# Gated cross-attention and routed feed-forward: mask and row maxima in one product of 115 rows, and a stationary first layer

## What is computed

```python
x = x + tanh(g_xattn) * xattn(layernorm(x), ctx, ctx, mask)        # 16 heads of 16
x = x + tanh(g_ffn) * ffn(layernorm(x))

# xattn: q, k, v = projections with biases
scores = einsum('bhqd,bhkd->bhqk', q, k) / sqrt(16)
scores = where(mask, -1e15, scores)
out = (softmax(scores) @ v) @ Wo + bo

# ffn: a router picks 3 of 8 zones for each image, with weights w that sum to 1
z = gelu(x @ Wa[e]) @ Wb[e]                                        # 256 -> 1024 -> 256
return x + sum over the three zones of z * w[e]
```

## Time and profile before

| | us |
|---|---|
| median of 3 runs (383.84 to 386.05) | 385.92 |
| the profiled execution | 384.96 |
| its span, first to last instruction | 383.2 |
| TensorE busy in it | 344.4 |
| VectorE, ScalarE, GpSimd busy | 177.0, 195.7, 158.5 |

### The profile page before, as it was taken

How to read it: one execution, slowest core, us unless ns; L and a number is a source line. 1 busy time by engine, 2 the same in 40 slices (tenths; PEclk the granted TensorE clock), 3 DMA queues, 4 the chain that set the end, 5 groups by cost and what they waited for, 6 DMA issues and landing times.

```text
span 383.2 us, 8751 instructions
## 1 busy us (share of the span) xinstructions
PE 344.4 (90%) x3060; PEld 267.8 (70%) x3060; DVE 177.0 (46%) x559; ACT 195.7 (51%) x398; POOL 158.5 (41%) x219
## 2 busy tenths in 40 slices
PE   2775896997999989989998878999999999999995
PEld 2542674875767768767776655888788887888875
DVE  4337455375475684765859352233332222222221
ACT  3334565564565657656775665344553434344341
POOL 4946767368466596674988681000000000000000
PEclk9968999899999999999999899999999999999999
DMA  7967648259367476572664130110101010101000
GB/s 171 280 182 198 173 120 235 86 139 208 106 174 196 126 211 178 145 220 70 191 173 138 60 118 3 35 38 24 38 2 38 0 39 2 39 0 38 2 12 14
DMA packets 32921, 40.40 MB, mean 105 GB/s; under 512 B 9992, under 2 KB 26688, under 8 KB 32880
## 3 DMA queue, kind: packets, MB, share of 16 engines
q1 hardware_dynamic: 26176, 22.07, 22.5%
q0 software_dynamic: 4784, 16.98, 15.1%
q10 hardware_dynamic: 1920, 0.79, 0.8%
HBM read 33.09 MB, written 6.74 MB: 104 GB/s over the span
## 4 chain that ended last, share of the span: by engine, by line
PE 71%; DMA 7%; DVE 7%; POOL 5%; issue 3%; ACT 3%; SPq 2%; ACTq 0%
PE bank L1184 17%; PE bank L1156 16%; PE bank L1020 5%; PE bank L1012 5%; PE bank L1166 5%; PE bank L970 4%; PE bank L960 4%; PE bank L994 3%; DMA stage<-in_L_ffn_Wa 3%; PE bank L980 3%; PE bank L974 3%; POOL wa L445 3%; PE bank L1037 2%; DVE bank L745 2%; DMA stage<-in_L_ffn_Wb 2%
## 5 line engine op out<-in xcount | busy, mean ns | idle before, releaser
L745 DVE CUSTOM_DVE_ANT_0 bank<-bank,maskb 112x375 f32<-112x375 f32 x128 | 67.8, 569 | 36.6 <-PE bank L960 36.5
L912 DVE SCALAR_TENSOR_TENSOR stage<-bank,wbc,stage 128x448 f16<-128x448 f32 x48 | 32.8, 684 | 85.8 <-ACT stage L708 85.8
L1156 PE MATMUL bank<-wa,ctxT 128*112 x288 | 70.0, 379 | 2.1 <-issue 2.1
L1184 PE MATMUL bank<-wb,stage 128*112 x576 | 67.0, 273 | 1.2 <-DVE stage L912 1.2
L1184 PEld LDWEIGHTS bank<-wb,stage 128*112 128x112 f16 x576 | 63.4, 130 | 4.1 <-issue 1.4
L527 ACT ACTIVATE pT<-bank 125x448 f32<-125x448 f32 x96 | 49.1, 539 | 21.9 <-PE bank L980 21.7
L708 ACT ACTIVATE stage<-bank,wbc 128x448 f16<-128x448 f32 x48 | 30.2, 630 | 54.3 <-PE bank L1166 54.2
L1156 PEld LDWEIGHTS bank<-wa,ctxT 128*112 128x112 f16 x288 | 35.7, 130 | 19.1 <-issue 2.3
L445 POOL TENSOR_TENSOR wb<-stage,wb 128x512 f16<-128x512 f32 x32 | 36.7, 1157 | 22.3 <-ACT wb L626 22.2
L445 POOL TENSOR_TENSOR wa<-stage,wa 128x512 f16<-128x512 f32 x32 | 36.7, 1156 | 21.8 <-ACT wa L626 21.6
L960 PE MATMUL bank<-kst,qbd 128*112 128x375 f16 x128 | 36.0, 344 | 10.3 <-DVE peaks L745 7.1
(11 more groups left out here) (113 smaller groups left out, 440.8 us busy)
## 6 DMA issues: line engine op xcount, KB each, us to landing
stage<-in_L_ffn_Wa POOLq DMA_DIRECT2D x16, 512.0 KB, 4.9
stage<-in_L_ffn_Wb POOLq DMA_DIRECT2D x16, 512.0 KB, 5.5
kst<-k_scr SPq DMA_DIRECT2D x64, 93.8 KB, 3.5
k_scr<-k_hl SPq DMA_DIRECT2D x16, 187.5 KB
ctx_s<-in_ctx SPq DMA_DIRECT2D x8, 336.0 KB
qbd<-q_scr SPq DMA_DIRECT2D x32, 56.0 KB, 3.2
xa<-in_x SPq DMA_DIRECT2D x8, 112.0 KB, 2.6
q_scr<-q_hl SPq DMA_DIRECT2D x32, 28.0 KB
```

Of the source, the lines that this page charges most:

```text
L745: v.tensor_tensor_reduce(out=bank[0:SQ, e, 0:SK], in0=bank[0:SQ, e, 0:SK], in1=maskb[:, b % 2, 0:SK], scale=-1.0, scalar=3.0e38, op0=ALU.a ...
L1156: ins = T.matmul(o, x2b[:, b % 2, xs * DT * SQ + t * SQ:xs * DT * SQ + (t + 1) * SQ], wa[:, bass.ds(e * (4 * CHUNK) + ws * (2 * CHUNK) + t ...
L1184: ins = T.matmul(o, hT[:, hs * FT * SQ + f * SQ:hs * FT * SQ + (f + 1) * SQ], wb[:, bass.ds(e * (4 * CHUNK) + ws * (2 * CHUNK) + f * D, D) ...
```

## The change

- **Mask and maxima in one product.** The mask tile gets three rows of ones below its 112, and the moving operand `rq` (115 rows, 448 columns, two buffers) holds four identities side by side and, below them, three rows with the maxima's parts of the four heads. The four products with `pick` go. The three rows lie on other partitions than the 12 transposed ones, so SyncE writes `ms` to DRAM (`write_max`) and reads three rows of it into `rq` for each group of tiles (`move_max`).
- **First scores a slot ahead.** Pairs 0 and 1 of image n now stand in slot 0 of iteration b, pairs 6 and 7 in slot 3. `row_max`, `split_max` and MX0 move with them; K0 and K1 come before Q; `mask_bias` moves to slot 3 of the iteration before.
- **Fully masked rows.** The negated minimum starts at 1e14 instead of 3e38, a floor. `vp` and `pT` get a 126th row in the last third: the row of V sums (times 2^-100) against a row of ones. For it the two copies of the transposed context also accumulate their row sums into column 376 (the one of VectorE becomes a multiply with accumulation).
- **First layer stationary.** VectorE copies the chosen zone's 4096 fp16 columns of `wa` to a fixed place, `wst3` and `wst1` (the attention weights' and part of `qbd`'s memory), and `g1(u)` streams x (112 columns) against 48 stationary blocks of 128 x 128. The result is already transposed, in four banks taken in turn; `ht` goes. ScalarE's gelu reads it to `h_w` and a second activation makes the high half (`hidden`), VectorE the low (`low`). `hT` has two buffers. TensorE's order is g1(u+1), g2(u). The last step of an image is done one unit later (`put_out`).

The diff, cut to its core:

```diff
     every = (
-        (("V0", n), ("XT", m), ("V1", n), ("MX1", b), ("CX0", m), ("CX1", m)),
-        (("Q", m), ("OT", o), ("K0", m), ("K1", m), ("X2T", b - 2)),
-        (("ON", o),),
-        (("MX0", n), ("OP", o)),
+        (("V0", n), ("XT", m), ("V1", n), ("CX0", m), ("CX1", m), ("MX1", b)),
+        (("K0", m), ("K1", m), ("Q", m), ("OT", o), ("X2T", b - 2)),
+        (("MX0", n), ("ON", o)),
+        (("OP", o),),
     )
...
+            def write_max(b, h):
+                if there(b):
+                    sp.wait_ge(s["ms_done"], 2 * b + h + 1)
+                    sp.dma_start(m_scr[b, h, :, :, :], ms[:, :, :]).then_inc(s["m_written"], 16)
+
+            def move_max(b, g):
+
+                if there(b):
+                    sp.wait_ge(s["m_written"], 16 * (2 * b + g // 2 + 1))
+                    need(sp, s["pe_st"], tile(b, g, 0) - KC)
+                    sp.dma_start(rq[SQ:KQ, g % 2, :].rearrange("c (j q) -> c j q", j=4),
+                                 m_scr[b, g // 2, :, g % 2, :].rearrange("(c j) q -> c j q", j=4)).then_inc(rq_in[g % 2], 16)
...
             sp.dma_start(wqkvo[:, 2, :, :], view_w(Wv)).then_inc(s["wv_loaded"], 16)
             for b in range(-2, B):
                 n, m, o = b + 1, b + 2, b - 1
+                move_max(b, 1)
                 read_q(n, 1)
                 read_k(n, 1)
                 load_xr(o)
                 load_mask(m)
                 load_x(m + 1)
-
+                write_max(b, 1)
                 load_ctx(m + 1)
+                move_max(b, 2)
+                write_k(m, 0)
+                write_k(m, 1)
+                move_max(b, 3)
                 write_q(m)
                 store_r(b - 2)
-
-                write_k(m, 0)
-                write_k(m, 1)
                 store_x2(b - 2)
+                write_max(n, 0)
...
+                read_k(m, 0)
                 read_q(m, 0)
-                read_k(m, 0)
+                move_max(n, 0)
...
-            def gelu(u, hf):
-
-                act.wait_ge(s["g1_done"], u * 2 + hf + 1)
-                need(act, s["ht_full"], u * 2 - 1 + hf)
-                a.activation(h_f[:, hf * 512:(hf + 1) * 512], bank[0:SQ, hf, :], ACT.Gelu_apprx_tanh,
-                             scale=1.0 / WSCALE).then_inc(s["gelu_done"], 1)
-
-            def ht_hi(u, hf):
-                if hf == 0:
-                    act.wait_ge(s["wbc_done"], 1 if u // TOPK < ROUTES[1][0] else 2)
-                act.wait_ge(s["ht_full"], u * 2 + hf + 1)
-                need(act, s["g2_done"], u)
-                a.activation(hT[:, hf * 448:hf * 448 + 448], bank[:, 2 + hf, 0:448], ACT.Copy,
-                             scale=wbc[:, u:u + 1]).then_inc(s["hthi_done"], 1)
+            def hidden(u):
+
+                act.wait_ge(s["wbc_done"], 1 if u // TOPK < ROUTES[1][0] else 2)
+                need(act, s["g2_done"], u - 1)
+                for hf in range(2):
+                    act.wait_ge(s["g1_done"], 2 * u + hf + 1)
+                    need(act, s["htlo_done"], 2 * u - 1 + hf)
+                    cols = slice(hf * QUAD, (hf + 1) * QUAD)
+                    a.activation(h_w[:, cols], bank[:, 2 * (u % 2) + hf, 0:QUAD], ACT.Gelu_apprx_tanh, scale=1.0 / WSCALE).then_inc(s["gelu_done"], 1)
+                    act.wait_ge(s["gelu_done"], 2 * u + hf + 1)
+                    a.activation(hT[:, u % 2, cols], h_w[:, cols], ACT.Copy, scale=wbc[:, u:u + 1]).then_inc(s["hthi_done"], 1)
...
             for b in range(-2, B):
                 n, m, o = b + 1, b + 2, b - 1
-                row_max(b, 6)
-                row_max(b, 7)
-                split_max(b, 1)
+                row_max(n, 0)
+                row_max(n, 1)
                 cx_copy(m)
                 if b == B - 1:
                     route_logits(0)
 
-                row_max(n, 0)
-                row_max(n, 1)
-                if b == -2:
-                    dve.wait_ge(s["wq_scaled"], 2)
-                q_lo(m)
-                o_rows(o)
-                if b == -2:
-                    dve.wait_ge(s["bk_loaded"], 16)
-                k_lo(m, 0)
-                result(b - 2)
-                k_lo(m, 1)
-                if b == B - 1:
-                    route_top(0)
-
                 row_max(n, 2)
                 row_max(n, 3)
                 split_max(n, 0)
+                if b == -2:
+                    dve.wait_ge(s["wq_scaled"], 2)
+                    dve.wait_ge(s["bk_loaded"], 16)
+                k_lo(m, 0)
+                k_lo(m, 1)
+                q_lo(m)
+                o_rows(o)
+                result(b - 2)
+                if b == B - 1:
+                    route_top(0)
+
+                row_max(n, 4)
+                row_max(n, 5)
                 x2_lo(b - 2)
                 ln1_stats(m + 1)
 
-                row_max(n, 4)
...
+            def copy_weights(u):
+
+                if u == ROUTES[1][0] * TOPK:
+                    dve.wait_ge(s["idx_loaded"], 32)
+                e = dve.value_load(idx_row[0:1, u:u + 1], min_val=0, max_val=NZ - 1)
+                need(dve, s["g1_done"], 2 * u)
+                v.tensor_copy(wst3, wa[:, bass.ds(e * (4 * CHUNK), 3 * CHUNK)]).then_inc(s["wst_done"], 1)
+                v.tensor_copy(wst1, wa[:, bass.ds(e * (4 * CHUNK) + 3 * CHUNK, CHUNK)]).then_inc(s["wst_done"], 1)
+
+            def low(u):
+                dve.wait_ge(s["wbc_done"], 1 if u // TOPK < ROUTES[1][0] else 2)
+                for hf in range(2):
+                    dve.wait_ge(s["hthi_done"], 2 * u + hf + 1)
+                    cols = slice(hf * QUAD, (hf + 1) * QUAD)
+                    v.scalar_tensor_tensor(out=hT[:, u % 2, (2 + hf) * QUAD:(3 + hf) * QUAD], in0=h_w[:, cols], scalar=wbc[:, u:u + 1],
+                                           in1=hT[:, u % 2, cols], op0=ALU.mult, op1=ALU.subtract).then_inc(s["htlo_done"], 1)
+
...
+            dve.wait_ge(s["idx_loaded"], 16)
+            dve.wait_ge(s["hi_done"], NPART)
+            dve.wait_ge(s["lo_done"], NPART)
+            full(dve, ("V1", B - 1))
+            dve.wait_ge(s["pe_st"], tile(B - 1, 0, 0))
+            copy_weights(0)
             for u in range(B * TOPK):
                 b, k = u // TOPK, u % TOPK
-                if k == 0:
-                    dve.wait_ge(s["wbc_done"], 1 if b < ROUTES[1][0] else 2)
-                for hf in range(2):
...
+                if u + 1 < B * TOPK:
+                    copy_weights(u + 1)
+                low(u)
...
-                    T.matmul(o[0:w, :].rearrange("k (j q) -> k j q", j=4), maskb[:, b % 2, c * CK:c * CK + w],
-                             bass.AP(ident_b, 0, [[SQ, SQ], [0, 4], [1, SQ]]), start=True, stop=False)
+                    if c == 0:
+                        pe.wait_ge(rq_in[g % 2], 16 * (2 * b + g // 2 + 1))
+                    T.matmul(o[0:w, :], maskb[0:KQ, b % 2, c * CK:c * CK + w], rq[0:KQ, g % 2, :], start=True, stop=False)
                     for i in range(2):
                         p = 2 * g + i
-                        T.matmul(o[0:w, i * 2 * SQ:(i + 1) * 2 * SQ].rearrange("k (e q) -> k e q", e=2),
-                                 kst[:, b % 2, p * SK + c * CK:p * SK + c * CK + w], qbd[:, b % 2, :, p, :],
-                                 start=False, stop=False)
-                    if c == 0:
-                        pe.wait_ge(s["ms_done"], 2 * b + g // 2 + 1)
-                    for j in range(4):
-                        ins = T.matmul(o[0:w, j * SQ:(j + 1) * SQ], pick[:, j, 0:w], ms[:, g, :],
-                                       start=False, stop=(j == 3))
+                        ins = T.matmul(o[0:w, i * 2 * SQ:(i + 1) * 2 * SQ].rearrange("k (e q) -> k e q", e=2),
+                                       kst[:, b % 2, p * SK + c * CK:p * SK + c * CK + w], qbd[:, b % 2, :, p, :],
+                                       start=False, stop=(i == 1))
                     ins.then_inc(s["pe_st"], 1)
...
             for b in range(-2, B):
                 for slot in range(4):
-                    n, p = (b, 6) if slot == 0 else (b + 1, 2 * slot - 2)
                     st_tile(b, slot, 0)
-                    s1(n, p)
+                    s1(b + 1, 2 * slot)
                     st_tile(b, slot, 1)
                     pv(b if slot else b - 1, (slot - 1) % COUPLES)
                     st_tile(b, slot, 2)
-                    s1(n, p + 1)
+                    s1(b + 1, 2 * slot + 1)
                     for name in slot_uses(b, slot):
...
-            def g1(u, e, hf):
+            def first(ws, t, f):
+                i = ws * DT + t
+                return wst3[:, i * CHUNK + f * 128:i * CHUNK + f * 128 + 128] if i < 3 else wst1[:, f * 128:f * 128 + 128]
+
+            def g1(u):
 
                 b, k = u // TOPK, u % TOPK
-                if k == 0 and hf == 0:
+                if k == 0:
                     pe.wait_ge(x2b_loaded[b % 2], 16 * (b // 2) + 16)
-                need(pe, s["gelu_done"], u * 2 - 1 + hf)
-                o = bank[0:SQ, hf, :]
```

(35 more changed lines are left out.)

168 lines of the change are left out of this document (95 added, 73 removed).

## The result

| | before | after |
|---|---|---|
| median of the runs (range) | 385.99 us (383.84 to 387.86) | 397.01 us (394.97 to 397.76) |
| profiled span | 383.2 us | 396.0 us |
| first tile of scores | 39.05 us | 50.72 us |
| slot 0 of image 6 begins | 189.04 us | 219.71 us |
| first feed-forward product | 230.80 us | 262.75 us |

The changed kernel is slower, by a ratio of 1.0285 (95% interval 1.0231 to 1.0339). Some executions of any of these kernels fall in a slower state: medians are of all runs, ratios of the others alone. 366 was forecast, so 31 us are missing, and the table says where: the feed-forward stage gave 19.1 us of the 24, and the attention stage cost 32 us where +6 was expected.

What follows compares the result with a forecast made beforehand. TensorE was taken to bound both stages, with a loop of DMAs close behind in attention. Attention +6 and feed-forward -24 on the profiled 384.96 us gave 366 us; its own range was 361 to 373, the wider one 350 to 380.

Steps and rivals of the forecast that it cites:

- the 24: Feed-forward stage: first layer without transposes, a unit of 4.94 us instead of 5.99, 24 us saved in all.
- +6: Attention stage in all: start +8, six iterations +2, end -4, so 6 us longer.
- rival (d): Feed-forward first layer paced by weight loads, 80 ns a product: +11 instead of -23, 402 us; chance 0.06.
- rival (e): Feed-forward weight copy goes by elements, 4.7 us, VectorE becomes the bound, 7.1 us a unit: 416 us; chance 0.08.
- by bytes: Feed-forward weight copies on VectorE, timed by bytes rather than elements: 2.6 us, just hidden behind the second layer.
- The stall itself: Attention, before slot 0: TensorE waits for the maxima, last in SyncE's queue, a new 3.6 us an iteration.
- the chain of 6.5 us from the end of x2_lo: SyncE's queue before slot 0: x2 store, maxima write, k and q reads, maxima read landing, 6.5 us.
- The clock: Attention: TensorE at half clock after stalls, 1.7 us lost each, in five of six iterations, 8.5 us.
- The rest of the iteration: Attention slots shortened by removed maxima products: 6.5, 6.75, 3.3 and, with the stall, 7.7, 24.2 us against 25.0.
- The end: From slot 0 of image 6 to the first feed-forward product: products removed, maxima waits and first copy added, -4 us.
- (c): Attention: maxima for slots 2 and 3 also late under weight traffic, +12 to +18: 378 to 385 us; chance 0.10.
- the eight small terms of the queue: Attention: the stall's length is a sum of eight small terms of SyncE's queue, named the likeliest error.

Runs made afterwards that it cites:

- e12: e7 with expert numbers stored ahead of x2 and the first weight copy ahead of a residual, in the last iteration: 363.9 us, ratio 0.9423 to the kernel before.
- e7: Kernel before with only the change's feed-forward parts, and two weight parts prepared in every slot, where slot 3 had one: 369.6 us, ratio 0.9653.
- e2: Changed kernel with the maxima left out of the scores and their two transfers through DRAM removed: 387.82 us, ratio 1.0073 to the kernel before.
- e9: Changed kernel with 64 unread products on TensorE just before it waits for slot 0's maxima: 389.41 us, ratio 1.0095 to the kernel before.
- e17: Kernel before with next x's factors at the start of slot 3 (GpSimd) and its normalisation behind slot 0's third exponential (ScalarE): 375.92 us, ratio 0.9707.
- e11: Kernel before with new feed-forward stage, 115-row product fed by transposes to partitions 96 to 98 without DRAM, smaller exponential and moving-tile rings: 372.7 us, ratio 0.9679.
- e18: Changed kernel with nothing but the normalisation order of e17: 396.26 us, ratio 1.0249 to the kernel before.
- e10: e2 with q ahead of k throughout, and stores of residual and x2 behind the reads of both in all iterations but the last: 375.18 us, ratio 0.9689.
- e14: e11 with the early first weight copy of e12, two weight parts in every slot and the order of e17: 353.57 us, ratio 0.9161.
- e13: e12 with the normalisation order of e17: 353.12 us, ratio 0.9175 to the kernel before.

## Why the prediction was wrong

**Feed-forward: right in mechanism and unit, 5 us short.** The first layer takes 2.36 us (2.32 forecast; 48 times 48 ns is 2.30), 49 ns a product, so rival (d) fell. The two copies take

```profile
L943 DVE COPY wqkvo<-wa 128x3072 f16 x24 | 23.2, 965 | 42.7 <-PE bank L1214 38.3 <-issue 4.3
L944 DVE COPY qbd<-wa 128x1024 f16 x24 | 10.1, 419 | 0.0
```

0.965 + 0.419 = 1.38 us and are hidden in most units; rival (e) fell. The bound "by bytes" of 2.6 us was twice too dear. By the Trainium skill (VectorE: DVE Perf Modes, The perf-mode tier table) it would have been an estimated 1.3; the trace agrees. The second row of the wait list has 10.9 us for the copy. 6.3 of them stand ahead of the first product and count below, under the end of attention. The missing part of this stage is the other 4.6, in four early units, where VectorE's leftover work of attention stands ahead of the copy, and the first unit's clock: its 48 products take 4.65 us at a granted clock of 0.50. The forecast hid the copy behind the second layer alone and did not ask what else is queued ahead of it. e12 took back the wait ahead of the first product (4.0 us in e7) by order; 4.9 us in four waits stay in it.

**Attention: +32 where +6 was forecast.** The terms, by the timeline: first tile 50.72 for 47 (+3.7), six iterations 169.0 for 151.7 (+17.3), slot 0 of image 6 to the first feed-forward product 43.0 for 41.8 - 4 = 37.8 (+5.2); 26 together, and 5 of the feed-forward stage make the 31. (The 366 are the profiled execution's; the 1.0 us by which the prediction puts the median above it was not added.)

- *The stall itself* was foreseen, with its place and its queue, at 3.6 us; it is 4.6. The step that failed is the chain of 6.5 us from the end of x2_lo: it holds no landing of a write. "Write of maxima 0.35" counts only the issue, and the write of q, which must land before its read, is not in the sum at all, though the maxima's read stands behind that read. By the pieces above, the landing of q's write (3.85 to 5.29 us) came last in four of the seven stalls, the first tile's among them, and the maxima's own write in one: 4.08 + 3.38 us there, where the sum has 0.35 + reads issued meanwhile + 2.1. In the two others no landing of a write is in the chain, and from the store of x2 to the tile it still takes 7.9 and 7.4 us for 6.5, with 2.78 and 2.93 us for the maxima's read in place of 2.1. In b=5 x2_lo was even earlier than forecast (its store is issued 0.5 us into slot 3, not behind 1.2), and the 6.5 us became 8.0. e2 shows the missing term by itself: without any maxima in DRAM q's write takes 5.8 us to be readable, and 3.8 us of each stall stay. The Trainium skill (DMA: Bandwidth & Descriptors, Anatomy of one DMA — SWDGE (gpsimd) path) puts the fixed cost of a transfer that GpSimd issues at about 2.0 us, most of it the receipt of the write in memory; SyncE's pieces of the chain here, under the weights' traffic, are 4.1 and 3.4 us for 5.2 and 2.6 KB, and they count twice in a round trip.
- *The clock* was right in mechanism and near in size: 8.5 us in six iterations were forecast, for five stalls of six; it fell behind all seven, and e9 got 7.3 back over the whole stage.
- *The rest of the iteration.* 28.2 less a stall of 4.6 and about 1.2 of clock leaves 22.4 us of slots, against 20.6 forecast (21.9, if the half clock is taken at 1.7). This is the larger part of the +17.3: six times 1.8, where the longer stall makes six times 1.0. That the removed products would shorten each slot by their full time assumed that TensorE alone set the pace. e17 shows that it did not in the kernel before, e11 that removing them brings nothing even without a stall. This was the premise read off and the earlier trace rows: the gap of 0.82 us was seen, put down to "an exp late on ScalarE", and not followed to its cause. In the changed kernel that cause is not the same one, since e18 is worth nothing. In b=5 slots 1 and 2, at full clock, take 7.51 and 3.82 us for 6.75 and 3.3; 0.50 of it is the wait for an exponential shown above. The rest of the 1.8 us was not taken apart. The sum was also built on b=5, one of the shorter iterations, without its gap: the 8.5 us for which TensorE waits for exponentials in the six iterations before were dropped without a reason. That they shrink to 2.4 us in the changed kernel, behind the stalls, was luck.
- *The end.* The waits of 2 and 3 us for the maxima's trips that were forecast here did not come. Against that, TensorE stands 6.3 us before the first feed-forward product, where 1.5 to 2 was forecast: the first copy waits for GpSimd's last weights, done at 259.99, and is issued at 261.18. A wait of 2.04 us for VectorE's row maxima stands in the last slots, and after it TensorE runs at half the clock again for 3.4 us.

**The rivals.** (c), more stalls, was the nearest in mechanism, with 378 to 385 us and a chance of 0.10; it placed the extra waits before slots 2 and 3, where one of 2.05 us stands in the first iteration and later ones stay at 0.2 to 0.5, and 397 lies beyond it. (d), at 402, is nearer in number only: its mechanism is not there. The slower side was given to two feed-forward mechanisms alone (0.14); none of attention reached it, although the prediction itself named the eight small terms of the queue as the place where it would be wrong most easily.

**What stays open.** Why the write of q takes 3.9 to 5.8 us and that of the maxima 4.1 was not taken apart (small pieces, or the weights' traffic: the DMA share is 0.65 in these windows). e10 still waits for k; no run had all three round trips relieved. And 0.8 to 1.3 us of each iteration's slots, above, have no shown cause.

## What to carry to other kernels

Count a value that goes through DRAM as two landings in a row, each from the last issue, and each at what a trace of the loaded chip shows; then look which queue stands still between the two, because everything behind it is late as well. Before crediting an engine with removed work, follow even its small gaps to their cause: here two moved steps of other engines were worth 11 us, and the removal of all the maxima products nothing (e14 against e13). And when several transfers end close together, taking one away tells little; compare through a version in which none is needed.

## What the runs showed of the hardware

- A write of 5.2 KB to DRAM and the read of 2.6 KB from it took 4.08 and 3.38 us while the queues carried 186 GB/s; the last of four writes of q was readable 5.8 us after its issue in e2, and took 3.85 to 5.29 us in the changed kernel.
- 48 products of 128x128 two-byte weights and 112 columns in a row keep 49 ns each with a changing weight, so weight loads of 100 ns (mean) overlap. The Trainium skill (TensorE: Matmul & The Clock Gate, Back-to-back issue gap) has about 81 ns for sustained pairs with 128 columns; the traces do not agree: e9's 64 pairs with 128 columns take 3.74 us, 58 ns each.
- Behind each of seven waits of 4.05 to 5.28 us TensorE's granted clock was 0.50 for 3.4 to 3.7 us; with 64 unread products in each wait it stayed at 1.00 in the middle of attention (e9).
- 3072 two-byte values a partition are copied within SBUF in 965 ns by VectorE.
- Transposes of three columns to partitions 96 to 98 of PSUM, and a copy from there, work as a way across partitions without a DMA (e11, e14); the copy of 3x896 values takes ScalarE 909 ns, 3x448 takes 528 and 12x224 takes 346 (medians): the time follows the columns and not the partitions.
